# First attention of a decoder in 32 units of 512 score columns in place of 64 units of 256

## The reference

```python
qkv = hidden_states @ w_attn + b_attn          # 512 -> 3 x 512
q, k, v = jnp.split(qkv, 3, axis=-1)           # then reshaped to 32 heads of 16
scores = jnp.einsum('bqhd,bkhd->bhqk', q, k) * SCALE      # SCALE = 1 / 16
scores = jnp.where(causal[None, None], scores + bias[None], -jnp.inf)
attn = jax.nn.softmax(scores, axis=-1)
out = jnp.einsum('bhqk,bkhd->bqhd', attn, v).reshape(B, S, HIDDEN)
return out @ w_proj + b_proj
...
x = _layernorm(x + _L0_attn_ref(x, ...), axis=-1)
```

## Time and profile before

| | us |
|---|---|
| median of 3 runs | 1771.96 |
| lowest and highest | 1769.37, 1772.05 |
| the profiled execution | 1767.49 |
| its span, first to last instruction | 1765.6 |
| PE busy | 1661.4 (94%) |
| DVE busy | 1013.3 (57%) |
| ACT busy | 672.9 (38%) |
| POOL busy | 208.8 (12%) |

### The profile page before, as it was taken

How to read it: one execution, slowest core, us unless ns; L and a number is a source line. 1 busy time by engine, 2 the same in 40 slices (tenths; PEclk the granted TensorE clock), 3 DMA queues, 4 the chain that set the end, 5 groups by cost and what they waited for, 6 DMA issues and landing times. The chain is left out here.

```text
span 1765.6 us, 23975 instructions
## 1 busy us (share of the span) xinstructions
PE 1661.4 (94%) x8910; PEld 1326.2 (75%) x8910; DVE 1013.3 (57%) x2177; ACT 672.9 (38%) x1271; POOL 208.8 (12%) x153
## 2 busy tenths in 40 slices
PE   8897888999999999999899999999999999888998
PEld 6665667778778877877678778878878877666866
DVE  2779776776676567667641552453345246236745
ACT  2564532443334333343423432332333223426541
POOL 5306104000000000000124000000000000612330
PEclk9998998999999999999999999999999999999999
DMA  4002001110011011011011110110111010202231
GB/s 181 12 13 96 25 2 59 37 60 24 26 48 48 2 61 48 13 37 37 1 43 50 60 49 13 36 59 24 36 36 48 12 37 24 71 12 69 73 89 48
DMA packets 26182, 75.85 MB, mean 43 GB/s; under 512 B 3904, under 2 KB 4640, under 8 KB 25824
## 3 DMA queue, kind: packets, MB, share of 16 engines
q1 hardware_dynamic: 25696, 73.42, 13.1%
q0 software_dynamic: 384, 1.05, 0.2%
HBM read 72.36 MB, written 2.10 MB: 42 GB/s over the span
## 5 line engine op out<-in xcount | busy, mean ns | idle before, releaser
L83 PE MATMUL bankY<-sb_Dwo,sb_DoT 128*128 128x512 f32 x768 | 194.0, 402 | 0.3 <-DVE sb_DoT L997 0.3
L83 PE MATMUL bankY<-sb_Bwo,sb_BoT 128*128 128x512 f32 x768 | 193.7, 401 | 0.3 <-DVE sb_BoT L997 0.3
L83 PE MATMUL bankA<-sb_xT,sb_Bwq 128*128 128x512 f32 x768 | 192.0, 400 | 0.0
L83 PE MATMUL bankA<-sb_xT,sb_Dwq 128*128 128x512 f32 x768 | 189.9, 396 | 0.0
L83 PEld LDWEIGHTS bankY<-sb_Dwo,sb_DoT 128*128 128x128 f32 x768 | 141.0, 189 | 42.3 <-issue 13.3
L83 PEld LDWEIGHTS bankY<-sb_Bwo,sb_BoT 128*128 128x128 f32 x768 | 141.0, 189 | 42.1 <-issue 12.9
L83 PEld LDWEIGHTS bankA<-sb_xT,sb_Bwq 128*128 128x128 f32 x768 | 143.7, 190 | 34.7 <-issue 3.0
L83 PEld LDWEIGHTS bankA<-sb_xT,sb_Dwq 128*128 128x128 f32 x768 | 142.2, 188 | 33.9 <-issue 2.7
L928 DVE TENSOR_TENSOR sb_BqT<-bankA,sb_Btable 128x512 f32<-128x512 f32 x64 | 44.2, 691 | 153.1 <-ACT sb_Bsw L830 153.1
L964 DVE TENSOR_TENSOR sb_xtok<-sb_xtok,bankY 128x512 f32<-128x512 f32 x128 | 87.2, 681 | 54.6 <-PE bankY L83 54.5
L830 ACT ACTIVATE sb_Bsw<-bankA 64x512 f32<-64x512 f32 x160 | 94.7, 592 | 54.9 <-PE bankA L83 51.7
(11 more groups left out here) (265 smaller groups left out, 3143.4 us busy)
## 6 DMA issues: line engine op xcount, KB each, us to landing
sb_raw<-in_w_attn SPq DMA_DIRECT2D x80, 512.0 KB, 3.5
sb_raw<-in_q_gu SPq DMA_DIRECT2D x22, 256.0 KB, 2.7
sb_raw<-in_q_d SPq DMA_DIRECT2D x11, 256.0 KB, 2.7
sb_rawx<-in_xT SPq DMA_DIRECT2D x4, 512.0 KB, 7.0
sb_raw<-in_wqk SPq DMA_DIRECT2D x8, 256.0 KB, 2.7
sb_xtok<-in_x_tok SPq DMA_DIRECT2D x1, 2048.0 KB, 13.4
sb_raw<-in_ctxT SPq DMA_DIRECT2D x4, 512.0 KB, 3.8
sb_raw<-in_ctx_tok SPq DMA_DIRECT2D x4, 512.0 KB, 3.9
```

What stands on the lines that cost most here:

```text
L83: last = nc.tensor.matmul(out, lhs, rhs, start=start and i == 0, stop=stop and i == len(pairs) - 1)
```

## The change

The first attention is written anew; nothing else is touched but the layout of four small inputs.

- A unit is now a chunk and two sequences (one token tile) with all 8 heads: 32 units. Keys are moved twice: ACT moves a half into `kt`, the upper 64 rows with the two sequences swapped, and four scalings by `own` write them into `kd` with one head kept in each 64-row half. Queries go to `qz`, half zero. A score matmul contracts 128 rows, of which 16 count as before, but all of its 256 columns now count: two matmuls a unit fill one bank with 8 heads of 64 keys. The softmax steps are the same, on 512 columns and 8 rows of maxima.
- `V` is laid out by chunk, sequence and head pair, with zeros in half of it (cleared by DVE for the lower 64 rows, by POOL for the upper), so that the context, 8 matmuls of 64 columns that contract 128 rows, comes out complete: no gather, no `parity`. ACT moves it once, with the value bias, to `first_o` or over the used part of `V`.
- V's banks are moved in quarters, the even ones by DVE, the odd ones by ACT.
- The context of chunks 0 to 2 is split (`split_early`, `low_early`) one unit ahead of the unit that ends the tile, and multiplied with 9 of the 12 output matmuls (`output_early`); the last chunk's part follows (`split` of it by `move` and `low_last`, then `output_last`).
- The output bias is added to x by DVE, ahead of its moves of V, and no longer by POOL. POOL's order of blocks puts three of the four context blocks behind the first q/k pair, and `wp` behind the second.

```diff
-    QUADS = B // 4
-    PER_CHUNK = QUADS * 4
-    UNITS = KC * PER_CHUNK
+    UNITS = KC * NT
...
-    OUTPUT_AT = UNITS - PER_CHUNK + 6
+    LAST_CHUNK = UNITS - NT
     AHEAD = 3
...
+        V = sb(mem, "AV", [P, KC, B, P])
...
+        kd = [sb(mem, f"Akd{h}", [P, NT, 4, S]) for h in range(2)]
+        oS = [[sb(mem, f"AoS{i}{p}", [P, KC, P], F32R) for p in range(2)] for i in range(2)]
+        qz = [sb(mem, f"Aqz{h}", [P, KC, 4, S]) for h in range(2)]
+        kt = sb(mem, "Akt", [P, KC, 2, S])
+        first_o = sb(mem, "AfirstO", [P, NT, P])
...
-        blocks += [(io["wqk"][c, a], [w[:, a].rearrange("p k n -> p (k n)") for w in wqk]) for c in range(KC) for a in range(2)]
-        blocks += [(io["wp"][:, i * BLK:(i + 1) * BLK], [w[:, i * BLK:(i + 1) * BLK] for w in flat(wbig)]) for i in range(2)]
-        blocks += [(io["ctxT"][:, k, :], [c[:, k, :] for c in cT]) for k in range(KC)]
+        order = [("v", k) for k in range(KC)] + [("qk", 0), ("qk", 1), ("c", 0), ("c", 1), ("c", 2), ("qk", 2), ("qk", 3), ("p", 0), ("p", 1)]
+        order += [("qk", i) for i in range(4, 2 * KC)] + [("c", 3)]
...
-                    if n == KC + 3:
-                        pool.wait_ge(small, 128)
-                        pool.wait_ge(in_tok, 16)
-                        for t in range(NT):
-                            nc.gpsimd.tensor_tensor(xtok[:, t, :], xtok[:, t, :], bp[:], ALU.add).then_inc(pbias, 1)
...
+                    if n == KC + 1:
+                        pool.wait_ge(zeroed, 4)
+                        pool.wait_ge(w_low, n + 1)
...
                 def scores(n):
-                    c, quad, m = slot(n)
+                    c, h, pr = slot(n)
...
+                    for a in range(2):
+                        done = nc.tensor.matmul(bankA[n % 2][:, a * 256:(a + 1) * 256], qz[h][:, pr, 2 * a:2 * a + 2, :].rearrange("p f s -> p (f s)"),
+                                                kd[h][:, 2 * pr + a].rearrange("p j k -> p (j k)"), start=True, stop=True)
+                    done.then_inc(s_ready, 1)
+
+                def attend(n):
+                    c, bp_ = n // NT, n % NT
...
+                    for a in range(2):
+                        for e in range(2):
+                            for jj in range(2):
+                                b, m = 2 * bp_ + e, jj + (0 if a == e else 2)
+                                at = (2 * a + jj) * P + e * S
+                                done = nc.tensor.matmul(bankO[32 * m:32 * m + 32, n % 2, e * S:(e + 1) * S], V[:, c, b, 32 * m:32 * m + 32],
+                                                        pt[n % 2][:, at:at + S], start=True, stop=True)
+                    done.then_inc(o_ready, 1)
...
+                def output_early(t):
+                    if t == 0:
...
+                    pe.wait_ge(e_low, 2 * (t + 1))
+                    product(bankY[t % 2][:], [x for k in range(KC - 1) for x in three([w[:, k, :] for w in oS[t % 2]], [w[:, k, :] for w in wbig])], stop=False)
+
+                def output_last(t):
+                    pe.wait_ge(o_low, t + 1)
+                    product(bankY[t % 2][:], three([w[:, KC - 1, :] for w in oS[t % 2]], [w[:, KC - 1, :] for w in wbig]), start=False).then_inc(y_ready, 1)
...
-                    for j in range(2):
-                        done = nc.tensor.transpose(bankT[n % 2][:, j * P:(j + 1) * P], sc[n % 3][:, j].rearrange("p b k -> p (b k)"), ident[:])
...
+                    for i in range(4):
+                        done = nc.tensor.transpose(bankT[n % 2][:, i * P:(i + 1) * P], sc[n % 3][:, 2 * i:2 * i + 2, :].rearrange("p j k -> p (j k)"), ident[:])
                     done.then_inc(t_ready, 1)
                     if n + AHEAD < UNITS:
                         scores(n + AHEAD)
-                    if c + 1 < KC:
-                        project(c + 1, n // 4 % 4, [n % 4])
-                    if n >= OUTPUT_AT:
-                        output((n - OUTPUT_AT) // 2, n % 2)
...
+                    if n < LAST_CHUNK:
+                        project(n // NT + 1, n % NT // 2, (range(0, 2), range(2, 4))[n % 2])
+                    else:
+                        output_early(n - LAST_CHUNK)
+                        if n > LAST_CHUNK:
+                            output_last(n - LAST_CHUNK - 1)
+                    attend(n)
+                output_last(NT - 1)
...
+                def values(t):
...
+                def keys(c, h):
...
+                    nc.scalar.activation(kt[LOW], src[LOW], ACT.Identity, bias=bqk[LOW, 1, c:c + 1]).then_inc(k_moved, 1)
+                    for e in range(2):
+                        nc.scalar.activation(kt[HIGH, :, e, :], src[HIGH, :, 1 - e, :], ACT.Identity, bias=bqk[HIGH, 1, c:c + 1]).then_inc(k_moved, 1)
...
+                    for j in range(4):
+                        nc.scalar.activation(kd[h][:, :, j, :], kt[:].rearrange("p r e s -> p (r e) s"), ACT.Copy, scale=own[:, j:j + 1]).then_inc(k_done, 1)
...
+                def queries(c, h):
...
+                    nc.scalar.activation(qz[h][LOW, :, 0:4:3, :], src[LOW], ACT.Identity, bias=bqk[LOW, 0, c:c + 1]).then_inc(q_done, 1)
+                    for e in range(2):
+                        nc.scalar.activation(qz[h][HIGH, :, 2 - e, :], src[HIGH, :, e, :], ACT.Identity, bias=bqk[HIGH, 0, c:c + 1]).then_inc(q_done, 1)
...
+                def move(n):
...
+                    src = bankO[:, n % 2, 0:P]
+                    if n < LAST_CHUNK:
+                        nc.scalar.activation(V[:, c - 1, t, :] if c else first_o[:, t, :], src, ACT.Identity, bias=bv[:, c:c + 1]).then_inc(o_done, 1)
+                    else:
+                        if t >= 2:
+                            act.wait_ge(y_ready, t - 1)
+                        nc.scalar.activation(oS[t % 2][0][:, c, :], src, ACT.Identity, bias=bv[:, c:c + 1]).then_inc(o_high, 1)
+
+                def split_early(t):
...
+                    nc.scalar.activation(oS[t % 2][0][:, 0, :], first_o[:, t, :], ACT.Copy).then_inc(e_high, 1)
+                    nc.scalar.activation(oS[t % 2][0][:, 1:KC - 1, :], V[:, 0:KC - 2, t, :], ACT.Copy).then_inc(e_high, 1)
...
+                act.wait_ge(small, 112)
+                for t in range(1, NT, 2):
+                    values(t)
...
+                for h in range(2):
+                    keys(0, h)
+                    queries(0, h)
...
+                    nc.scalar.activation(pt[n % 2][:], bankT[n % 2][:], ACT.Copy).then_inc(pt_done, 1)
+                    if n:
+                        move(n - 1)
+                    if n == UNITS - 2:
+                        ln_roots(act, 0, 0)
                     if n + 2 < UNITS:
...
+                    if n % 2 == 0 and 2 <= n <= LAST_CHUNK:
+                        c, i = (n - 2) // NT + 1, (n - 2) % NT // 2
+                        (queries if i % 2 else keys)(c, i // 2)
+                    if n >= LAST_CHUNK - 1 and n - LAST_CHUNK + 1 < NT:
+                        split_early(n - LAST_CHUNK + 1)
+                move(UNITS - 1)
                 ln_rest(act, 0)
...
+                nc.vector.memset(v_blocks(LOW, 1), 0.0).then_inc(v_zero, 1)
...
+                def low_early(t):
...
+                    nc.vector.tensor_tensor(oS[t % 2][1][:, 0, :], first_o[:, t, :], f32(oS[t % 2][0][:, 0, :]), ALU.subtract).then_inc(e_low, 1)
+                    nc.vector.tensor_tensor(oS[t % 2][1][:, 1:KC - 1, :], V[:, 0:KC - 2, t, :], f32(oS[t % 2][0][:, 1:KC - 1, :]), ALU.subtract).then_inc(e_low, 1)
+
+                def low_last(t):
...
+                    nc.vector.scalar_tensor_tensor(oS[t % 2][1][:, KC - 1, :], bankO[:, t % 2, 0:P], bv[:, KC - 1:KC], f32(oS[t % 2][0][:, KC - 1, :]),
...
-                dve.wait_ge(small, 128)
...
+                dve.wait_ge(in_tok, 16)
                 for t in range(NT):
+                    nc.vector.tensor_tensor(xtok[:, t, :], xtok[:, t, :], bp[:], ALU.add).then_inc(pbias, 1)
+                for t in range(0, NT, 2):
                     values(t)
...
-                    in_turns(gather(n // 4 - 1) if n % 4 == 0 and n else None, front(n + 2) if n + 2 < UNITS else None, back(n + 1) if n + 1 < UNITS else None)
-                    if n % 4 == 1 and n > 4:
...
+                    if n > LAST_CHUNK:
+                        low_last(n - LAST_CHUNK - 1)
+                    in_turns(front(n + 2) if n + 2 < UNITS else None, back(n + 1) if n + 1 < UNITS else None)
+                    if n >= LAST_CHUNK - 1 and n - LAST_CHUNK + 1 < NT:
+                        low_early(n - LAST_CHUNK + 1)
+                    if n > LAST_CHUNK:
+                        residual(n - LAST_CHUNK - 1)
+                low_last(NT - 1)
+                residual(NT - 1)
```

More of the change, by code:

```diff
@@ L228, in build_program @@
-        bqk = sb(mem, "Abqk", [P, 2, KC]); bp = sb(mem, "Abp", [P, D])
+        alibi = sb(mem, "Aalibi", [P, KC, D])
+        bqk = sb(mem, "Abqk", [P, 2, KC]); bv = sb(mem, "Abv", [P, KC]); bp = sb(mem, "Abp", [P, D])
```

(20 more changed lines are left out.)

237 lines of the change are left out of this document (106 added, 131 removed).

## The result

The changed kernel takes **1708.1 us** (median of 4 runs, 1705.7 to 1710.6) beside 1770.7 for the one before: ratio 0.966, 95% interval 0.965 to 0.968. The forecast was 1719.5, range 1701 to 1738: right in sign and range, and 11 us too careful.

| us | before | after | moved | forecast |
|---|---|---|---|---|
| start, to the first transposes | 50.2 | 55.24 | +5.0 | +6.8 |
| loop, to the transposes of the first unit without projections | 149.65 | 93.15 | -56.5 | -50.3 |
| last chunk, to the last residual addition | 60.1 | 55.48 | -4.6 | -9.0 |
| all behind it, to the span's end | 1505.6 | 1501.3 | -4.3 | 0 |

The account below looks back on a forecast made before the run. The prediction took TensorE to bound the first attention only in part, with VectorE held up by POOL. Start +6.8, loop -50.3 and last chunk -9.0 gave -52.5, so 1715.0 for the execution and a median of 1719.5 us, range 1701 to 1738.

Parts of the forecast that it names:

- I take the issue rate seen ... 69 ns: 1.1 us: Loop, context of a unit: 16 instructions at 69 ns, 1.1 us; bounds 0.55 with strips overlapping, 1.6 at full passes.
- Rival (a): Everything hides better: column strips overlap (0.55 us a context) and the clearing holds nothing; about 1703 us, chance 0.15.
- the keys' 1.8 us: Loop: delay from the keys' copies on ACT, 0.3 us six times.
- POOL's 2 us: Loop: 2 us for blocks POOL still splits beside it, two of `wp` at its head above all.
- (c): Slower than before: small context matmuls don't pipeline, 4.5 us a context; 1828 us, chance 0.05 with other losers.
- the term was 0 for 4: Start: bias additions held up by POOL's clearing make the first projection 4 us late, middle of 0 and 8.
- DVE's 5.75 us: Last chunk: DVE's work in a full unit, taken as the bound there over PE's 5.4 us.
- rival (b): Last chunk: DVE waits for ACT's context move, unit 7.5 us, +9; with costlier keys and late start 1737 us, chance 0.15.
- The tail's new wait: End of last chunk: `residual(6)` stands ahead of `low_last(7)` on DVE, its roots behind ACT's four scalings, 2.93 us.
- The stall of 3.3 us: Last chunk: ACT's 3.3 us wait on "remote" beside the rope gathers stays.
- the last step: From execution to median: 1715.0 us became 1719.5, as the old execution lay 4.5 us under its median.
- The point on the scores: Scores issued three units ahead are no rival but no gain either, since `AHEAD` is 3 on both sides.

Follow-up runs that it names:

- one_strip: Changed kernel with all eight context matmuls of a unit writing the first 32 rows of the bank, one column strip instead of four: 1708.8 us (one run).
- before_pool_order: Kernel before the change, with only GpSimd's block-splitting order taken from the changed kernel: 1765.8 us, 0.9993 of the kernel before.

## Why the prediction was right, and where it wasn't

**The loop** was 6.2 us better than its 99.3. The step "I take the issue rate seen ... 69 ns: 1.1 us" for the context was the wrong one, and its lower bound too: 0.36 us, 23 ns an instruction, under the 0.55. The row it took, two row halves at a time, has two blocks working beside each other; here there are four strips. Rival (a) had the mechanism, overlap of the four strips: the scores' 1024 columns take 0.68 us and these 1024 take 0.36, and `one_strip` agrees. The Trainium skill (TensorEngine Tiling (Array Packing), Key Properties) says that different tiles can execute in parallel; the trace agrees. Its Instruction Overhead, an estimated 0.8 us, is not seen in the four-strip group (0.36); that in one strip takes 1.02.
The scores were put at 0.81 and took 0.68, the projections 1.67 for 1.59: a unit of 3.20 for 3.98, 18.6 us in 24 units. But two terms beside it were too small: the keys' 1.8 us are 8.6, since at 3.20 ACT's lump no longer hides (the forecast gave it until 2.9 us into the unit) and the queries wait for it too; and POOL's 2 us are 7.6 with the clock's share in three units. -18.6 + 6.8 + 5.6 = -6.2. So that the loop came within 6.2 us is partly luck: an error of 18.6 us was met by 12.4 us the other way. The 2 us for POOL rested on the new order being worth 11 us, and `before_pool_order` gave 5.6. `one_strip` says what the context's price was really worth: 3 us, as a slower unit hides part of the other two. Rival (a) in full would have been 1703; the 6.8 us of waits for ACT are the largest term against it. (c) fell by far: 23 ns against the 170 from which it decides.

**The start** was 1.8 us better. The clearing holds no addition: the last five followed each other every 0.60 us beside it. The three before, beside the splitting of the q/k block, took 1.24, 1.45 and 1.70 us, which makes the 7.48 in place of the 4.9 put for eight alone. The nearest row (1.44 us beside a clearing) misled. The Trainium skill (SBUF — State Buffer, Who interferes with whom) has it that a DVE instruction with two SBUF inputs contends with a GpSimd instruction that reads SBUF, not with one that only writes; the trace agrees. So the term was 0 for 4; not foreseen was that V's product ended later, so that the projections began at 33.2 and not 31.9; from the first scores to the first transposes it took 10.3 for 9.8, for the reason named, wp's blocks.

**The last chunk** was 4.4 us worse. DVE's 5.75 us were 5.64, but the unit 6.24: the high parts queue on ACT behind an exponential that waits for DVE. The forecast named a round trip as rival (b), through another instruction (the context move) and at 9 us; the one that came was worth 0.6 a unit. Of the 4.4 us, 2.5 lie in the five middle units, 1.1 in the last two, 0.6 in the tail and 0.2 in the stall. The tail's new wait was right: 5.25 forecast from the last context move to the last addition, 5.8 measured (198.06 to 203.87). The stall of 3.3 us stayed, 3.15; that it came out so near is luck, since it ran from 0.25 to 4.67 in the other kernels.

**What lay behind** was carried over at 0 and moved by 4.3 us. The code is the same, and in the 14 kernels profiled its length runs from 1497.5 to 1505.6. The largest piece is in the middle of the next attention (PE's timeline and a window of before, then PE's timeline of after):

```profile
618.72 1.65 PE L752 MATMUL bankA<-sb_Bkt,sb_BqT 128*128 128x128 f32 x6 [2.12 <-issue]
...
621.45 4.92 PE L83 MATMUL bankA<-sb_xT,sb_Bwq 128*128 128x512 f32 x12
```
```profile
618.00:622.00 4.00, 3.28 (x11) 2.36 (x12) 2.61 (x7) 0.97 (x2) 0.00 (x0) 0.59 0.14 18
```
```profile
561.91 0.48 PE L827 MATMUL bankO<-sb_Bpt,sb_BV 64*128 64x256 f32 x1 [0.59 <-issue]
562.32 3.05 PE L83 MATMUL bankA<-sb_xT,sb_Bwq 128*128 128x512 f32 x12
```

Before, TensorE stood still for 2.12 us with no wait that the profile shows, and ran on at a lower clock (mean granted 0.59 in the window); after, it stood for 0.59 and kept its clock. From one pair of transposes to the next that is 10.21 us (616.00 to 626.21) against 5.79 (559.42 to 565.21), which alone makes up the 4.3. What sets the length of such a pause stays open; no run here was made for it. Of the 60.5 us between the profiled executions, then, 56.1 lie in the code that was changed; that the other 4.3 are the change's doing, nothing here shows.

Of the 11.4 us between forecast and median, these parts make some 8 (6.2 + 1.8 - 4.4 + 4.3). The other 3.4 come from the last step: the forecast put the median 4.5 us over its execution, as before, and the changed kernel's lies 1.1 over its own. The 4.3 behind the change widened the miss by about what the last chunk's 4.4 took off it.

**The point on the scores** (three ahead: no gain) was right as a difference, since both kernels have it, but it undersold it: at two ahead the new unit loses 32 us.

## What to carry to other kernels

When a unit gets shorter, price again what used to hide in it: a lump on a side engine (4.1 us on ACT here) costs nothing until the unit is shorter than its slack, and then it costs in two places (8.6 us of this loop). An engine busy 3.14 of 3.20 us has no cover left: what contends with it costs by the operations it meets, and the same block cost 6.1 us in the changed kernel and 2.1 with the keys spread. Single gains don't add up when one of them moves what another removes. Many short matmuls are cheap when they go to different column strips; all in one strip they took nearly three times as long here.

## What the runs showed of the hardware

- Sixteen matmul instructions of 64 columns and their weight loads: 0.36 us in four column strips, 0.38 with both of a strip behind each other, 1.02 in one strip.
- A TensorE pause can cost more than its length: after waits of 4.07 and 1.79 us the next twelve products took 4.69 and 5.49 us in place of 3.02; after a wait of 1.91 us, at 162.75 in the changed kernel, they took 3.01.
- Beside GpSimd's splitting operations on 1024 columns a 0.69 us VectorE subtraction or multiplication takes 2.2 to 2.9 us, while reductions and operations from PSUM keep their 0.68; beside its 3.5 us clearing, additions go on every 0.60 us.
- A stall of ACT beside indirect gathers, put down to "remote", was 0.25 us in one kernel, 4.67 in another, and between in ten more; 3.15 and 4.58 in two that differ only in the order of their context matmuls. Its cause is open.
